# Layer-norm of the next batch in a turned layout: x also turned on the host, the row statistics sent once through DRAM, and VectorE's steps reordered

## The chip, the cores and the metric

One core of one Trainium2 chip. The metric is the device time of one execution, in microseconds (us); lower is better. Engines are named as the profile names them: PE (TensorE), DVE (VectorE), ACT (ScalarE), POOL (GpSimd), SP (SyncE, here only a DMA queue).

## What is computed

```python
def _layernorm(x, axis=-1, eps=1e-05):
    m = jnp.mean(x, axis=axis, keepdims=True)
    v = jnp.var(x, axis=axis, keepdims=True)
    return (x - m) / jnp.sqrt(v + eps)
# attention(e, q): e is the normed x, q the context of 77 rows
Sim = (e @ w1)[:, :, None] + (q @ w2)[:, None, :] + einsum('bid,bjd->bij', e * w3, q) + b_sim[0]
A = softmax(Sim, axis=2);  hq_hat = einsum('bij,bjd->bid', A, q)
Batt = softmax(max(Sim, axis=2), axis=1);  hc_bar = einsum('bi,bid->bd', Batt, e)
hcq = concat([e, hq_hat, e * hq_hat, e * hc_bar]) @ W_qv + b_qv
x = x + attention(layernorm(x), ctx)
# ffn(e): hidden = e @ W1 + b1; a sine term of hidden is added; relu; @ W2 + b2
x = x + ffn(layernorm(x))
```

x is 16 batches of 512 rows by 512 features, in float32; the FFN is 2048 wide. The first layer-norm is called LN1 here, the one before the FFN LN2.

## The kernel before, in words

A float32 product is made from three products of split operands (a high part rounded to fp32r and a low part, the rest): the PE helper `three` (L513 to L515) issues high by high, high by low and low by high. So each operand of the PE needs a high part, a copy by ACT, and a low part, a subtraction by DVE (the helper `low`, L1045).

**The pipeline over batches.** After an opening (`attention_first`) for batch 0, `body(b)` runs the FFN of batch b in 16 steps f = 0 to 15 and beside it the attention of batch n = b + 1. Each engine has a program of its own with the same loop; the order within a step is written out by hand, and semaphores tie the engines. In step f PE runs `hidden(f)` (12 matmuls of 512 columns into `hid`) and `second(f - 3)` (12 into `acc`). ACT reads `hid` twice (phase, L868; h, L871), makes the high part of the relu (L877) and the sine (L881). DVE reduces the phase (L1167, L1169), adds the sine term (`sine_term`, L1159) and makes the relu's low part (`relu_low`, L1173), which first waits for ACT's L877.

**The attention of n beside it.** Step 0 and 1: PE turns the normed rows `xin1` of batch n, 16 transposes of 128 by 128 (`tr_first`, helper line L615); ACT copies each from PSUM twice (L797 to the high part of T, L804 to `full`), DVE makes T's low part. Step 1 to 3: the context's parts, `sim_column` (L1151), and `sim` on PE ahead of `hidden(3)`. ACT adds the bias (`sim_bias`, L886) ahead of its phase of step 3, PE turns the result (`sim_rows`, L636) directly behind `hidden(3)`. Steps 4 to 7: row maxima, softmax, the row mean. Step 8: `prob_turn` on PE. At the start of step 9 ACT and DVE copy its result to `at_s` (`stack_out` L906, `second_stack_out` L1214), and PE reads it in `hq_hat(n, 0)` (L521, L522) between `hidden(9)` and `second(6)`. At step 10 PE runs `hidden(10)`, `hidden(11)` and the whole product with W_qv (`products`); DVE waits there for PE's chunks (`chunk`). Steps 11 to 15: x plus attention, statistics, LN2, eight transposes each at steps 13 and 14 (`tr_second`).

**LN1 of the batch after.** SP loads `xin1` (`xin_load`) at step 1 and X at step 6; DVE takes the statistics of n + 1 at step 3 (`stats_first`, L1058), POOL turns them into mean and 1/std (`deviation_first`, L1520 to L1532) at step 4, DVE applies them by rows at step 10 (`norm_first`, L1062).

**Queues.** POOL issues all loads of split weights (`w1_load`, `tile_load`), each behind a wait for PE; SP issues loads of x and of the context (`ctx_load`, L409), and the stores. In body 0 the weights are split for the first time: raw loads on SP, high parts by ACT (L861, L853), low parts by DVE (`w1_low`, `tile_low`), stores by POOL. There PE's `hidden(f + 2)` waits for DVE's `w1_low` of step f.

Of the kernel before, what the change touches and what calls it, by code (L numbers as in the profile page):

```python
# [37 lines left out]
P = 128  # L38
# [12 lines left out]
def xattn_ffn(nc, x, ctx_rows, w_sim, b_sim, W_qv, b_qv, W1, b1, theta, w_real, w_imag, W2, b2, out):  # L51
# [32 lines left out]
    g_dram = nc.dram_tensor("g_dram", [CN, P, C, CR], F32).ap()  # L84
    hqw_dram = nc.dram_tensor("hqw_dram", [B * J, D], F32).ap()

    with ExitStack() as ctx:
# [21 lines left out]
        X = sb("X", [P, 2, RT, D])  # L109
        xin1 = sb("xin1", [P, RT, D])  # L110
# [26 lines left out]
        e_bc = sb("e_bc", [P, R])  # L137
        hqs = sb("hqs", [P, 2, D], F32R)
# [15 lines left out]
        mv = sb("mv", [P, RT, 3]); mv_x = sb("mv_x", [P, RT, 3])  # L154
# [6 lines left out]
        rstd = sb("rstd", [P, RT]); rstd_x = sb("rstd_x", [P, RT])  # L161
# [36 lines left out]
        ctx_in = sem("ctx_in"); x1_in = sem("x1_in"); xin_in = sem("xin_in"); x_in = sem("x_in")  # L198
# [143 lines left out]
        c_product = [X[:, 1, q] for q in range(4)]  # L342

        w1q_raw, w1q = w3_sb, T[:, 1]

# [10 lines left out]
        def _(sp):  # L356
            row = lambda v, n: v.rearrange("(a d) -> a d", a=1).to_broadcast([n, D])

            def xin_load(n):

                sp.wait_ge(tr1, RT * n)
                sp.dma_start(xin1[:], x_rows[n]).then_inc(xin_in, 16)

            def x_load(n, par):

                need(sp, out_stored, 16 * (n - 1))
                sp.dma_start(X[:, par], x_rows[bass.ds(n, 1)].rearrange("b p t d -> (b p) t d")
                             ).then_inc(x_in, 16)
# [96 lines left out]
            def store(b, par):  # L465
                sp.wait_ge(b_evac, RT * (b + 1))
                sp.dma_start(out_rows[bass.ds(b, 1)].rearrange("b p t d -> (b p) t d"), X[:, par]
                             ).then_inc(out_stored, 16)

            def attention_first():  # L470
                for q in range(2):
                    sp.wait_ge(g_stored[3 + q], g_stores(3 + q, CN))
                    raw_w1_load(q)

            def body(b, par, first, last):
                n, pn = b + 1, 1 - par
                for f in range(FT):
# [14 lines left out]
                    if f == 1 and n + 1 < B:  # L492
                        xin_load(n + 1)
                    if f == 6:
                        if first:
                            for q in range(4):
                                sp.wait_ge(p_late[q], 16)
                        x_load(n, pn)

            def rest():  # L500
                for t in range(RT):
                    sp.wait_ge(b_evac, RT * (B - 1) + t + 1)
                    sp.dma_start(out_rows[B - 1, :, t], X[:, (B - 1) % 2, t]).then_inc(out_stored, 16)
# [6 lines left out]
        def _(pe):  # L510
# [107 lines left out]
            def tr_first(n, t):  # L618

                transpose_rows(n, t, xin1[:, t], xn1, tr1, (t2_lo, RT * n - 2 + t + 1) if t < 2 else (t1_lo, RT * n + t - 1))  # L620
# [77 lines left out]
            def attention_first():  # L698
                pe.wait_ge(s_ident, 1)
                turn(0)  # L700
                turn_vectors()
                turn(1)
                multiply(0)
# [25 lines left out]
                multiply(7)  # L729
                tr_second(0, 0)  # L730
# [6 lines left out]
            def body(b, par, first, last):  # L737
                n, pn = b + 1, 1 - par
                for f in range(FT):
                    if f == 3 and not last:  # L740
                        sim(n, pn)
# [31 lines left out]
                    if last:  # L773
                        continue
                    if f == NA + 3:
# [18 lines left out]
        def _(sc):  # L794
            def turned_high(n, t, par, ready, done):
                sc.wait_ge(ready, RT * n + t + 1)
                nc.scalar.copy(T[:, par, 0, :, t * P:(t + 1) * P],  # L797
                               mis[:, t % 2].rearrange("p (c r) -> p c r", c=C)).then_inc(done, 1)

# [124 lines left out]
            def attention_first():  # L924
# [41 lines left out]
                w1_high(1)  # L966
                product_copy(7)
# [67 lines left out]
        def _(ve):  # L1035
# [11 lines left out]
            def stats_first(n, t):  # L1047
# [4 lines left out]
                else:  # L1052
                    if n == 1:
                        ve.wait_ge(x1_in, 16)
                    else:
                        ve.wait_ge(xin_in, 16 * (n - 1))
                    ve.wait_ge(xn1, RT * n)
                    ve.bn_stats(st_x[:, t], xin1[:, t]).then_inc(st1, 1)  # L1058

            def norm_first(n, t):  # L1060
                ve.wait_ge(rs1, n + 1)
                ve.tensor_scalar(xin1[:, t], X[:, 0, t] if n == 0 else xin1[:, t], mv_x[:, t, 1:2],  # L1062
                                 rstd_x[:, t:t + 1], ALU.subtract, ALU.mult).then_inc(xn1, 1)
# [152 lines left out]
            def row_mean(n, chunks=range(C)):  # L1216

                for c in chunks:
                    ve.wait_ge(full_done, RT * (n + 1))
# [37 lines left out]
            def evacuate(par, t, done):  # L1257
                ve.tensor_tensor(X[:, par, t], X[:, par, t], acc[:, t], ALU.add).then_inc(done, 1)

            def attention_and_stats(n, par, tiles=range(RT)):  # L1260

                if n > 0:
                    ve.wait_ge(x_in, 16 * n)
                for t in tiles:
                    ve.wait_ge(att_done, RT * n + t + 1)
                    evacuate(par, t, x2_done)
                    ve.wait_ge(x2_done, RT * n + t + 1)
                    ve.bn_stats(st[:, t], X[:, par, t]).then_inc(st2, 1)

            def norm_second(n, par, t):  # L1270
# [3 lines left out]
                ve.tensor_scalar(xin[:, t % 2], X[:, par, t], mv[:, t, 1:2], rstd[:, t:t + 1],  # L1274
                                 ALU.subtract, ALU.mult).then_inc(xn2, 1)

            def add_b2(n, par, t):
# [3 lines left out]
                ve.tensor_tensor(X[:, par, t], X[:, par, t], b2_bc[:], ALU.add).then_inc(xb2_done, 1)  # L1281

            def add_first_part(b, par):
# [3 lines left out]
                for t in range(RT):  # L1287
                    evacuate(par, t, a_evac)

            def add_last_part(b, par, whole):  # L1290
# [6 lines left out]
                for t in range(RT):  # L1297
                    if whole:
                        ve.wait_ge(last_sum, t + 1)
                    evacuate(par, t, b_evac)  # L1300

            def attention_first():
# [11 lines left out]
                for t in range(RT):  # L1314
                    norm_first(0, t)
# [43 lines left out]
                for t in range(RT):  # L1359
                    norm_first(1, t)  # L1360
# [4 lines left out]
                for half in range(2):  # L1365
                    pair = range(2 * half, 2 * half + 2)
                    attention_and_stats(0, 0, pair)
                    variance_of(st, mv, vareps, 2 * half, 2 * half + 2, st2, ag2, va2)
                    for t in pair:
                        norm_second(0, 0, t)  # L1370
                for t in range(RT):
                    turned_low(0, t, 0, t2_hi, t2_lo)
                add_b2(0, 0, 0)
                add_b2(0, 0, 1)
                ve.wait_ge(g_stored[0], g_stores(0, CN))

            def body(b, par, first, last):
                n, pn = b + 1, 1 - par
                for f in range(FT):
                    g = FT * b + f  # L1380
                    if f == NA - 1 and not last:
                        second_stack_out(n)
# [4 lines left out]
                    if f == 1 and not last:  # L1387
                        turned_low(n, 0, pn, full_done, t1_lo)
                        turned_low(n, 1, pn, full_done, t1_lo)
                    if f == 2 and not last:  # L1390
                        turned_low(n, 2, pn, full_done, t1_lo)
                        turned_low(n, 3, pn, full_done, t1_lo)
                        g_low(n)
                        sim_column(n)
# [230 lines left out]
```

## Time and profile before

| what | value |
|---|---|
| median of 3 runs | 2024.87 us (2021.78 to 2025.04) |
| the profiled execution | 2022.12 us |
| its span, first to last instruction | 2020.3 us |
| granted TensorE clock, mean | 0.996 of full |
| busy: PE, DVE, ACT, POOL | 98%, 67%, 48%, 20% |
| DMA | 386 MB, 191 GB/s |

Two microseconds of the profiled time lie outside its span. In the views a duration is that of one instruction; instructions of PE overlap, so what one of them costs is the distance between two starts. "Idle" rows name what ended the wait.

### The profile page before, as it was taken

Reading aid. Unit: us, or ns where it says so; the run is one execution under the profiler, and the core shown is the slowest. Engines: PE = TensorE matmul, PEld = TensorE weight load, DVE = VectorE, ACT = ScalarE, POOL = GpSimd, SP = SyncE. Lnnn points to the kernel's source line nnn. Section 1 sums busy time; section 2 is a strip of 40 time slices with the busy share of each in tenths; the row PEclk is TensorE's granted clock in tenths of the full one; section 3 lists DMA queues with packets and bytes.
Section 4 is the critical chain, followed back from the end, with each engine's and each line's share of the span. In section 5 each row is a group of like instructions: output and inputs, shape, how many; then the busy total and the mean of one; then the engine's idle time right before and its main releaser. Section 6 shows DMA issues by size and latency. Waiting matters only on the chain.

```text
span 2020.3 us, 25250 instructions
## 1 busy us (share of the span) xinstructions
PE 1980.5 (98%) x9057; PEld 1626.0 (80%) x9057; DVE 1356.7 (67%) x2406; ACT 965.3 (48%) x1669; POOL 401.1 (20%) x834
## 2 busy tenths in 40 slices
PE   6989999999999999999999999999999999999999
PEld 5767788888888888888888888888888888888887
DVE  6777675767767577675767767567675767767554
ACT  7464543635445363543636445363543636445343
POOL 0122222212122121122212122121122212121110
PEclk9999999999999999999999999999999999999999
DMA  7375856757477574766757476574766756467473
GB/s 261 121 263 188 288 178 175 238 150 223 136 214 218 152 231 127 229 180 173 238 148 224 138 217 216 151 230 128 227 182 174 235 148 222 142 196 217 136 209 124
DMA packets 143679, 386.22 MB, mean 191 GB/s; under 512 B 24995, under 2 KB 34539, under 8 KB 143556
## 3 DMA queue, kind: packets, MB, share of 16 engines
q0 software_dynamic: 83584, 304.31, 49.9%
q1 hardware_dynamic: 59828, 80.27, 12.6%
q8 instruction: 73, 1.20, 0.3%
q14 instruction: 50, 0.41, 0.1%
q10 hardware_dynamic: 144, 0.04, 0.0%
HBM read 343.81 MB, written 40.76 MB: 190 GB/s over the span
## 4 chain that ended last, share of the span: by engine, by line
PE 71%; DVE 15%; ACT 7%; issue 5%; DMA 1%; SPq 0%; DVEq 0%; POOL 0%; ACTq 0%
PE acc L513 13%; PE acc L514 13%; PE acc L515 13%; PE hid L513 8%; PE hid L515 8%; PE hid L514 8%; DVE ph L1169 3%; DVE h L1159 3%; PE mis L615 3%; ACT act L877 2%; DVE kk L1167 2%; DVE st_x L1058 2%; DVE tmp_w L1221 1%; ACT L881 1%; PE mis L521 1%
## 5 line engine op out<-in xcount | busy, mean ns | idle before, releaser
L513 PE MATMUL hid<-T,w1s 128*128 128x512 f32 x1024 | 403.8, 394 | 4.9 <-DVE ws L1045 4.3
L513 PE MATMUL acc<-ws,act 128*128 128x512 f32 x1024 | 404.1, 395 | 0.0
L515 PE MATMUL hid<-T,w1s 128*128 128x512 f32 x1024 | 399.8, 390 | 0.0
L514 PE MATMUL acc<-ws,act 128*128 128x512 f32 x1024 | 399.4, 390 | 0.0
L515 PE MATMUL acc<-ws,act 128*128 128x512 f32 x1024 | 399.4, 390 | 0.0
L514 PE MATMUL hid<-T,w1s 128*128 128x512 f32 x1024 | 399.3, 390 | 0.0
L868 ACT ACTIVATE ph<-hid,hbias 128x512 f32<-128x512 f32 x256 | 176.0, 688 | 407.2 <-PE hid L515 407.2
L877 ACT ACTIVATE act<-h 128x512 fp32r<-128x512 f32 x256 | 161.9, 632 | 390.6 <-DVE h L1159 369.4
L1173 DVE SCALAR_TENSOR_TENSOR act<-h,act 128x512 fp32r<-128x512 f32 x256 | 177.3, 693 | 185.7 <-ACT act L877 185.7
L1167 DVE TENSOR_SCALAR kk<-ph 128x512 f32<-128x512 f32 x256 | 108.8, 425 | 284.0 <-ACT ph L868 284.0
L1498 POOL DMA_DIRECT2D ws<-w2x_dram x240 | 127.6, 532 | 750.1 <-PE acc L515 739.8
L513 PEld LDWEIGHTS hid<-T,w1s 128*128 128x128 f32 x1024 | 192.9, 188 | 45.2 <-DVE ws L1045 4.7
L515 PEld LDWEIGHTS hid<-T,w1s 128*128 128x128 f32 x1024 | 192.5, 188 | 40.7
L515 PEld LDWEIGHTS acc<-ws,act 128*128 128x128 f32 x1024 | 192.5, 188 | 40.4
L514 PEld LDWEIGHTS hid<-T,w1s 128*128 128x128 f32 x1024 | 192.9, 188 | 38.8
L1492 POOL DMA_DIRECT2D w1s<-w1x_dram x240 | 129.5, 539 | 475.6 <-PE hid L515 460.0
L513 PEld LDWEIGHTS acc<-ws,act 128*128 128x128 f32 x1024 | 192.8, 188 | 38.4
L514 PEld LDWEIGHTS acc<-ws,act 128*128 128x128 f32 x1024 | 192.8, 188 | 38.3
L1159 DVE SCALAR_TENSOR_TENSOR h<-ph,camp,h 128x512 f32<-128x512 f32 x256 | 190.9, 746 | 0.0
L1169 DVE TENSOR_TENSOR ph<-ph,kk 128x512 f32<-128x512 f32 x256 | 177.3, 693 | 8.8
L871 ACT ACTIVATE h<-hid,cols 128x512 f32<-128x512 f32 x256 | 174.6, 682 | 0.0
L881 ACT ACTIVATE ph<-ph 128x512 f32<-128x512 f32 x256 | 157.9, 617 | 0.2
(172 smaller groups left out, 2760.2 us busy)
## 6 DMA issues: line engine op xcount, KB each, us to landing
w1s<-w1x_dram POOLq DMA_DIRECT2D x240, 512.0 KB, 4.5
ws<-w2x_dram POOLq DMA_DIRECT2D x240, 512.0 KB, 4.0
ws<-wqx_dram POOLq DMA_DIRECT2D x56, 512.0 KB, 4.5
X<-in_x SPq DMA_DIRECT2D x15, 1024.0 KB, 8.7
out_x<-X SPq DMA_DIRECT2D x15, 1024.0 KB, 4.6
xin<-in_x SPq DMA_DIRECT2D x14, 1024.0 KB, 6.8
w_raw<-in_L_ffn_W SPq DMA_DIRECT2D x32, 256.0 KB, 4.6
w1x_dram<-w1s POOLq DMA_DIRECT2D x16, 512.0 KB, 3.6
```

Of the source, the lines that this page charges most:

```text
L513: pe.matmul(dst, w_hi, m_hi, start=start, stop=False)
L514: pe.matmul(dst, w_hi, m_lo, start=False, stop=False)
L515: mm = pe.matmul(dst, w_lo, m_hi, start=False, stop=stop)
L868: nc.scalar.activation(ph[:, f % 2], hid[:, f % 2], ACT.Identity, bias=hbias[:, f:f + 1], scale=HSCALE).then_inc(t_done, 1)
L871: nc.scalar.activation(h2[:, f % 2], hid[:, f % 2], ACT.Identity, bias=b1c[:, f:f + 1], scale=1.0).then_inc(h2_done, 1)
L877: nc.scalar.activation(act[:, f % 4, 0], h2[:, f % 2], ACT.Relu).then_inc(act_hi, 1)
L881: nc.scalar.activation(ph[:, f % 2], ph[:, f % 2], ACT.Sin, scale=TWO_PI_BELOW).then_inc(s_done, 1)
L1159: ve.scalar_tensor_tensor(out=h2[:, f % 2], in0=ph[:, f % 2], scalar=camp[:, f:f + 1], in1=h2[:, f % 2], op0=ALU.mult, op1=ALU.add).then_i ...
L1167: ve.tensor_scalar(kk[:], ph[:, f % 2], ROUND, -ROUND, ALU.add, ALU.add).then_inc(k_done, 1)
L1169: ve.tensor_tensor(ph[:, f % 2], ph[:, f % 2], kk[:], ALU.subtract).then_inc(r_done, 1)
L1173: ve.scalar_tensor_tensor(out=act[:, f % 4, 1], in0=h2[:, f % 2], scalar=0.0, in1=act[:, f % 4, 0].bitcast(F32), op0=ALU.max, op1=ALU.subtract
L1492: po.dma_start(w1s[:, s].rearrange("p a c k -> p (a c k)"), w1x_dram[f % FT].rearrange("p a c k -> p (a c k)")).then_inc(w1_in[s], 16)
```

## The change

The host also hands in x turned: `in_x_turned`, per batch 128 partitions by 4 chunks by 512 rows. For n from 1 to 15 the turned x is loaded straight into `full`, and LN1 is applied there by two passes over it, `center` and `scale`; mean and 1/std vary along the free axis there. So they are sent to all partitions: PE turns the 12 columns (mean, variance, 1/std of 4 tiles) in one transpose, ACT copies them out, SP stores them to DRAM and, after a wait for that store, loads mean and 1/std as 512-element rows to all 128 partitions (`mean_bc`, `e_bc`). X has three buffers; `xin1` is gone. Batch 0 keeps its transposes, its normed rows lie in `w0_sb`, whose load moves behind them. `multiply(0)` goes ahead of `turn(1)` in the opening.

```diff
 # SP
-            def xin_load(n):
-                sp.wait_ge(tr1, RT * n)
-                sp.dma_start(xin1[:], x_rows[n]).then_inc(xin_in, 16)
+            def turned_load(n):
+                sp.wait_ge(pr_lo, C * n)
+                sp.dma_start(full[:], x_turned[n]).then_inc(xt_in, 16)
+            def spread_stats(n):
+                sp.wait_ge(srow_done, n)
+                sp.dma_start(stat_dram[n % 2], srow).then_inc(stat_st, 16)
+                sp.wait_ge(stat_st, 16 * n)
+                sp.wait_ge(hbr_done, C * n)
+                for at, dst in ((0, mean_bc[:]), (2 * RT, e_bc[:])):
+                    sp.dma_start(dst, stat_dram[n % 2, at:at + RT].rearrange("(a t) p -> a (t p)", a=1).to_broadcast([P, R])
+                                 ).then_inc(bc_in, 16)
...
                     if f == 6:
...
+                        x_load(n + 1)
+                    if f == NA + 1:
+                        turned_load(n + 1)
+                    if f == NA + 2:
+                        spread_stats(n + 1)
 # PE
+            def turn_stats(n):
+                pe.wait_ge(rs1, n + 1)
+                pe.wait_ge(prt_done, C * n)
+                pe.transpose(mis[0:3 * RT, 1, 0:P], row_x[:, 1:4].rearrange("p k t -> p (k t)"), ident[:]).then_inc(srow_t, 1)
             def tr_second(n, t):
+                if t == 1 and n + 1 < B:
+                    pe.wait_ge(srow_done, n + 1)
...
-                    if f == 3 and not last:
-                        sim(n, pn)
                     if f != NA + 1 or last:
                         hidden(b, f, par)
                     if f == 8 and not last:
                         prob_turn(n)
-                    if f == 0 and not last:
-                        tr_first(n, 0)
-                        tr_first(n, 1)
-                    if f == 1 and not last:
-                        tr_first(n, 2)
-                        tr_first(n, 3)
                     if f == 3 and not last:
-                        sim_rows(n)
-                    if f == NA - 1 and not last:
-                        hq_hat(n, 0)
+                        sim(n, pn)
...
                         second(b - 1, FT + f - LAG, False, True)
                     if last:
                         continue
+                    if f == 3:
+                        sim_rows(n)
+                    if f == NA - 1:
+                        hq_hat(n, 0)
+                    if f == NA + 2 and n + 1 < B:
+                        turn_stats(n + 1)
 # ACT
+            def spread_high(n, c, par):
+                sc.wait_ge(xs_done, 4 * n)
+                nc.scalar.copy(T[:, par, 0, c], full[:, c]).then_inc(t1_hi, 1)
+            def stat_rows(n):
+                sc.wait_ge(srow_t, n)
+                need(sc, xs_done, 4 * (n - 1))
+                nc.scalar.copy(srow, mis[0:3 * RT, 1, 0:P]).then_inc(srow_done, 1)
...
-                    if f in (1, 2) and not last:
-                        for t in (2 * f - 2, 2 * f - 1):
-                            turned_high(n, t, pn, tr1, t1_hi)
-                            full_copy(n, t)
-                    if f == 3 and not last:
-                        sim_bias(n)
+                    if f == 1 and not last:
+                        spread_high(n, 0, pn)
+                        spread_high(n, 1, pn)
...
                     if f == 1:
+                        spread_high(n, 2, pn)
+                        spread_high(n, 3, pn)
                         g_high(n)
                     if f == 2:
                         context_high(n)
+                    if f == 3:
+                        sim_bias(n)
+                    if f == NA + 2 and n + 1 < B:
+                        stat_rows(n + 1)
 # DVE
+            def center(n, half):
+                if half == 0:
+                    ve.wait_ge(xt_in, 16 * n)
+                    ve.wait_ge(bc_in, 32 * n)
+                cs = slice(2 * half, 2 * half + 2)
+                ve.tensor_tensor(full[:, cs], full[:, cs], mean_bc[:].unsqueeze(1).to_broadcast([P, 2, R]), ALU.subtract
+                                 ).then_inc(xs_done, 1)
+            def scale(n, half):
+                ve.wait_ge(xs_done, 4 * n - 1 if half else 4 * n - 2)
...
+                ve.tensor_tensor(full[:, cs], full[:, cs], e_bc[:].unsqueeze(1).to_broadcast([P, 2, R]), ALU.mult
+                                 ).then_inc(xs_done, 1)
...
                     reduce_phase(b, f)
                     if f > 0 or not first:
                         sine_term(g - 1, (f - 1) % FT)
+                    if f == NA - 2 and not last:
+                        second_stack_out(n)
...
                     if f > 0 or not first:
                         relu_low(g - 1, (f - 1) % FT)
 # POOL
+                    if f == NA + 1 and n + 1 < B:
+                        deviation_first(n + 1)
                     weights(b, f, first, last)
...
-                    if f == 4 and n + 1 < B:
-                        deviation_first(n + 1)
```

DVE's new order within a step, where the diff is long: behind `sine_term` and ahead of `relu_low` now come, step by step, `scale` (0), `sim_column` and two `spread_low` (1), `add_b2` (3 and 4, all four tiles), `prob_low` and `row_mean` (6), `row_mean` and `context_low` (7), `second_stack_out` and `w0_chunk` (8), `pr_chunk` (10), `center` of n + 1 (15), and in body 0 all `w1_low` and `tile_low`. Step 2 begins with `g_low` and the other two `spread_low`. `stats_first` moves from step 3 to step 10, between the chunks; `norm_first` by rows is left for batch 0 alone. In body 0 the product additions of steps 0 and 1 (four in all) move to step 3.

## Rows read from the trace of the kernel before

**Rows 1.** The page, busy time: us, share, instructions of each engine
```profile
PE 1980.5 (98%) x9057; PEld 1626.0 (80%) x9057; DVE 1356.7 (67%) x2406; ACT 965.3 (48%) x1669; POOL 401.1 (20%) x834
```

**Rows 2.** Chain that ended last, 930 to 1130 us: start, us, engine, tile, line
```profile
939.22 0.87 PE mis L615 x8
...
954.62 0.87 PE mis L615 x8
...
1060.52 0.87 PE mis L615 x8
```

**Rows 3.** Timeline of PE, steps 8 and 9 of one body
```profile
1007.02 0.39 PE L513 MATMUL hid<-T,w1s 128*128 128x512 f32 x1
...
1009.52 0.39 PE L515 MATMUL hid<-T,w1s 128*128 128x512 f32 x1
1010.18 0.50 PE L521 MATMUL mis<-at_s,hqs 128*128 128x512 f32 x1 [0.28 <-DVE at_s L1214]
1010.52 0.39 PE L522 MATMUL mis<-at_s,hqs 103*128 103x512 f32 x1
```

**Rows 4.** Waits of PE, whole run: us in total, times, longest
```profile
PE mis L521 <- DVE at_s L1214: 9.7, 14, 6.1
...
PE hid L513 <- DVE ws L1045: 4.3, 1, 4.3
PE mis L513 <- DVE gs L1045: 3.6, 1, 3.6
...
PE mis L615 <- DVE T L1045: 2.5, 3, 2.1
```

**Rows 5.** Waits of PE from 226 us on, same columns
```profile
PE mis L521 <- DVE at_s L1214: 3.6, 13, 0.3
```

**Rows 6.** Timeline of DVE, step 3 of one body
```profile
976.30 0.43 DVE L1167 TENSOR_SCALAR kk<-ph 128x512 f32<-128x512 f32 x1 [1.88 <-ACT ph L868]
976.76 0.69 DVE L1169 TENSOR_TENSOR ph<-ph,kk 128x512 f32<-128x512 f32 x1
977.37 0.75 DVE L1159 SCALAR_TENSOR_TENSOR h<-ph,camp,h 128x512 f32<-128x512 f32 x1
978.82 0.69 DVE L1173 SCALAR_TENSOR_TENSOR act<-h,act 128x512 fp32r<-128x512 f32 x1 [0.70 <-ACT act L877]
979.43 2.47 DVE L1058 BATCH_NORM_STATS2 st_x<-xin 128x6 f32<-128x512 f32 x4
```

**Rows 7.** Timeline of ACT, steps 2 and 3 of the same body
```profile
971.22 0.62 ACT L881 ACTIVATE ph<-ph 128x512 f32<-128x512 f32 x1
971.74 0.61 ACT L845 CAST hqs<-ctx_raw 128x512 fp32r<-128x512 f32 x1
...
974.31 0.69 ACT L886 ACTIVATE tmp_w<-mis,vj 77x512 f32<-77x512 f32 x1
975.58 0.69 ACT L868 ACTIVATE ph<-hid,hbias 128x512 f32<-128x512 f32 x1 [0.59 <-PE hid L515]
976.17 0.68 ACT L871 ACTIVATE h<-hid,cols 128x512 f32<-128x512 f32 x1
978.16 0.63 ACT L877 ACTIVATE act<-h 128x512 fp32r<-128x512 f32 x1 [1.31 <-DVE h L1159]
```

**Rows 8.** Groups of DVE by shape: count, busy us, mean ns, idle before
```profile
L1045 DVE TENSOR_TENSOR T<-mis,T 128x512 fp32r<-128x512 f32 x128 | 84.7, 688 | 32.3 <-ACT full L804 21.4 <-ACT T L797 10.8
...
L1200 DVE TENSOR_TENSOR prob<-prob,rrec 128x308 f32<-128x308 f32 x16 | 7.7, 479 | 0.6
```

**Rows 9.** DMA issues: queue, count, KB each, median us to landing
```profile
X<-in_x SPq DMA_DIRECT2D x15, 1024.0 KB, 8.7
...
w_bc<-in_L_xattn_w_sim SPq DMA_DIRECT2D x1, 256.0 KB, 9.1
...
g_dram<-kk SPq DMA_DIRECT2D x1, 252.0 KB, 9.0
```

**Rows 10.** Timeline of ACT, step 12 of the same body
```profile
1046.95 0.69 ACT L868 ACTIVATE ph<-hid,hbias 128x512 f32<-128x512 f32 x1 [8.44 <-PE hid L515]
```

**Rows 11.** Stretches of body 0: PE, PEld, DVE, ACT, POOL busy, clock, DMA
```profile
106.00:110.00 4.00, 4.00 (x12) 2.62 (x11) 2.94 (x5) 3.27 (x7) 0.62 (x2) 0.59 1.01 326
...
222.00:226.00 4.00, 3.51 (x10) 2.84 (x11) 0.28 (x1) 0.00 (x0) 1.61 (x3) 0.59 0.75 241
```

More of the change, by code:

```diff
@@ L729, in attention_first @@
                 multiply(7)
+                turn_stats(1)
                 tr_second(0, 0)
@@ L1366, in attention_first @@
                     pair = range(2 * half, 2 * half + 2)
[L1367 removed]
+                    attention_and_stats(0, pair)
                     variance_of(st, mv, vareps, 2 * half, 2 * half + 2, st2, ag2, va2)
                     for t in pair:
[L1370 removed]
+                        norm_second(0, t)
                 for t in range(RT):
                     turned_low(0, t, 0, t2_hi, t2_lo)
[L1373 to L1374 removed]
+                for half in range(2):
+                    center(1, half)
                 ve.wait_ge(g_stored[0], g_stores(0, CN))
@@ L1386, in body @@
                         chunk_low(n, 0)
-                    if f == 1 and not last:
-                        turned_low(n, 0, pn, full_done, t1_lo)
-                        turned_low(n, 1, pn, full_done, t1_lo)
                     if f == 2 and not last:
-                        turned_low(n, 2, pn, full_done, t1_lo)
-                        turned_low(n, 3, pn, full_done, t1_lo)
                         g_low(n)
-                        sim_column(n)
+                        spread_low(n, 2, pn)
+                        spread_low(n, 3, pn)
                     if f == 4 and not last:
@@ L1407, in body @@
                         sine_term(g - 1, (f - 1) % FT)
+                    if f == NA - 2 and not last:
+                        second_stack_out(n)
+                    if first and f == 3:
+                        for k in range(GAP, CN):
+                            product_add(k)
+                    if first and f < FT - 2:
+                        w1_low(f + 2)
+                    if f == 0 and not last:
+                        scale(n, 0)
+                        scale(n, 1)
+                    if f == 1 and not last:
+                        sim_column(n)
+                        spread_low(n, 0, pn)
+                        spread_low(n, 1, pn)
@@ new lines, in body @@
+                    if f == FT - 1 and n + 1 < B:
+                        center(n + 1, 0)
+                        center(n + 1, 1)
+                    if f == 3:
+                        add_b2(b, 0)
+                        add_b2(b, 1)
+                    if f == 4:
+                        add_b2(b, 2)
+                        add_b2(b, 3)
+                    if f == 6 and not last:
+                        prob_low(n)
+                        row_mean(n, range(0, C // 2))
+                    if f == 7 and not last:
+                        row_mean(n, range(C // 2, C))
+                        context_low(n)
@@ L1408, in body @@
+                    if f == NA - 2 and not last:
+                        w0_chunk(n, 0)
+                    if f == NA and not last:
+                        pr_chunk(n, 1)
+                    if first:
+                        for p in splits(f, last)[0:1] if f == NA else splits(f, last):
+                            tile_low(p)
+                    if f > 0 or not first:
                         relu_low(g - 1, (f - 1) % FT)
                     if f == 2 and not first:
-                        add_last_part(b - 1, pn, False)
@@ L1411, in body @@
-                    if first and f < 2:
-                        product_add(GAP + 2 * f)
-                        product_add(GAP + 2 * f + 1)
-                    if first and f < FT - 2:
-                        w1_low(f + 2)
-                    if f == NA + 1 and first:
-                        for p in splits(f, last):
-                            tile_low(p)
-                    if f == 0:
-                        add_b2(b, par, 2)
-                        add_b2(b, par, 3)
+                        add_last_part(b - 1, False)
@@ L1461, in body @@
                         turned_low(n, 3, pn, t2_hi, t2_lo)
-                    if f not in (NA, NA + 1) and first:
-                        for p in splits(f, last):
-                            tile_low(p)
             def rest():
@@ L1581, in body @@
                         w1_store(f + 2)
-                    if first and f < 2:
-                        for k in range(GAP + 2 * f, GAP + 2 * f + 2):
+                    if first and f == 3:
+                        for k in range(GAP, CN):
                             late_product_out(k)
@@ L1619 @@
         args.append(nc.dram_tensor(f"in_{name}", a.shape, _mybir.dt.from_np(a.dtype), kind="ExternalInput").ap())
+    a = _np.asarray(inputs['x'])
+    a = _np.ascontiguousarray(a.reshape(a.shape[0], a.shape[1], -1, P).transpose(0, 3, 2, 1))
+    arrays["in_x_turned"] = a
+    args.append(nc.dram_tensor("in_x_turned", a.shape, _mybir.dt.from_np(a.dtype), kind="ExternalInput").ap())
     shape = inputs['x'].shape
```

138 lines of the change are left out of this document (63 added, 75 removed).

## Prediction

> **What bounds the kernel now.** I read the page first: PE is busy 98% of the span, DVE 67%, ACT 48% [rows 1]. A change has to shorten PE's own work or a wait of PE; relief of the others is worth nothing unless they end such a wait. The chain of waits gives the period: the same transposes of step 13 start at 939.22 and 1060.52, so a body takes 121.3 us [rows 2]. There are 14 full bodies of this kind (b = 1 to 14), body 0 before them and a last one without attention. Then PE's waits: 36 us in all, but from 226 us on only one kind is left, 13 times `at_s`, 0.3 us each [rows 4, 5]. The rest lies in the opening and in body 0 (6.1, 4.3, 3.6 and 2.1 us) [rows 4].
>
> **Prices on PE.** 11 steps from 1007.02 to 1009.52 make 0.227 us for a matmul of 512 columns, so `hidden` or `second` (12 of them) is 2.72 us [rows 3]. Eight transposes take 0.87 us, 0.109 each [rows 2]. That is the distance of starts. The Trainium skill (TensorE: Matmul & The Clock Gate, PE-mode transpose) gives about 275 ns for one transpose in a kernel; the sum by that price would take 4.4 us from each body and not 1.74, some 37 us more in all, and is too large if transposes overlap, as the row says.
>
> **The change part by part, for one body of the 14.**
>
> 1. The 16 transposes of `tr_first` go: 16 x 0.109 = **-1.74 us**. They are on PE's path in full, nothing waits there at that time [rows 5].
>
> 2. One transpose of 12 columns comes (`turn_stats`, step 12). The trace has none of this shape; between nothing and one full transpose with a refill of 0.2, I take **+0.11** (its moving side is the same 128 columns). Its waits are long over: statistics are taken between the chunks of step 10, where DVE is idle, and POOL's eight small instructions follow before step 12. Behind `deviation_first` on POOL now stand a W1 load and the four tile loads of step 11, some of which leave up to 9 us later; they are read from step 12 on. Its ACT copy waits some 5 us inside step 12, where ACT's next work is `hidden(13)`, later still.
>
> 3. The wait for `at_s` goes. PE is free at 1009.52 + 0.227 = 1009.75, L521 starts at 1010.18, and the next start is 0.34 behind it where 0.23 is normal: 0.43 + 0.11 = **-0.54 us** [rows 3]. Now `second(6)` (2.72 us) stands ahead of `hq_hat(n, 0)`, and `second_stack_out` is a step earlier, so some 4 us of slack are there.
>
> 4. DVE: relu_low stands idle for 0.70 us in nearly every step, waiting for ACT's L877 [rows 6]. The new order fills that gap with other work. In the full bodies this moves no PE work by itself; it is slack.
>
> 5. `center` and `scale`, two instructions each of 128x1024. One DVE instruction of 512 takes 0.69 us with starts 0.60 apart, one of 308 takes 0.48 [rows 8]; the slope is 1.02 ns per element, so 1024 elements cost 1.14 from start to start, with 0.6 (if twice the rate) and 2.3 (if half) as ends. I take 1.14: two of them 2.3 us in step 15 and 2.3 in step 0. Against them 4 `norm_first` are gone. DVE has the room on average.
>
> 6. The path of the statistics through DRAM. ACT's phase of step 12 starts at 1046.95 [rows 10]. PE is done with three `second` 8.2 us later, at 1055; store at 1055.6; `center` comes in step 15, behind `hidden(13)`, `second(10)`, 8 transposes, `hidden(14)`, `second(11)`, 8 transposes, `hidden(15)` and DVE's reduce and sine term, at about 1073. So 17 us stand ready for a store, a wait and two loads of 256 KB. The nearest rows, in the crowded opening, are 9.0 and 9.1 us [rows 9]: 19 us at worst, 5 or 6 if the queues are free. I take no cost: behind `center` on DVE stands `relu_low(14)`, which PE needs only in the next step 1, 5 us after its usual time. x turned (1 MB, 8.7 us [rows 9]) is asked for at the end of step 10 and has 30 us. `ctx_load` is now queued behind this on SP, some 14 us later than before, and still 20 us ahead of its use.
>
> 7. **The new wait.** Here I expect a part of the gain to be given back. Let A be ACT's start of the phase, step 0 at A = 0. By PE alone steps follow at 5.44 (two times 2.72). DVE: kk 0.72 after the phase, sine term at 1.79, two `scale` from 2.45 to 4.8. ACT's `spread_high` waits for both, so two copies (0.52 each) end at 5.85 and the phase of step 1 starts 0.4 late. From there: DVE's sine term at 7.66, relu high part 0.78 later at 8.44 [rows 6, 7], sine, two more `spread_high`, `g_high` from 10.54; DVE's `g_low` at 11.05, two `spread_low`, and only at 12.66 kk of step 2, one us late. Then, with distances of rows 6 and 7: relu high part at 14.51, sine, four context copies (2.57 us) to 18.14, the phase of step 3 (PE has had it ready since 16.3, since `sim` no longer stands ahead of `hidden(3)`), kk 18.86, sine term 19.93, relu high part 20.71, sine, and now `sim_bias` last, 21.77 to 22.46. PE has by then run `second(15)`, `hidden(3)`, `sim` (12 matmuls, 2.78) and `second(0)` and is at `sim_rows` at 21.78. It waits 0.72, and refilling costs the 0.11 of point 3: **+0.83 us**. Ends: none, if DVE or ACT gain 0.7 anywhere on this line, and 2 us if each instruction between is 5% dearer. I take the middle because every term is from a row.
>
> Sum for a body: -1.74 + 0.11 - 0.54 + 0.83 = -1.34 us; 14 times, **-18.8 us**.
>
> **Opening and body 0.** In the opening PE's `multiply(0)` fills a DMA wait, but ACT's parts of `turn(1)` come some 2 us later; the w0 load leaves later and w3's earlier. Ends -2 and +3, taken as 0. Body 0 is bound by DVE up to step 9. It loses 16 transposes and the 6.1 us at `at_s` [rows 4], since the relu gap of 0.7 us in some seven steps is filled and `at_s` is wanted later; but the same line as in point 7 makes PE wait at `sim_rows` some 5 us, and body 0 has shown that waits of 3.6 and 4.3 us are followed by four microseconds at a granted clock of 0.59, mostly at the lower of the two levels (1.2 GHz) [rows 4, 11]. The skill's same page warns of this in its table of goals, to avoid long idle gaps between bursts of matmuls; rows 11 agree. Following DVE's list step by step I get `products` of body 0 some 4.5 us earlier. The last wait (4.3 us, a tile's low part in step 15) stays: two `center` take the place of `relu_low` and two `add_b2` ahead of it, and SP's raw loads wait 3 us behind `spread_stats`. Together **-4 us**, ends -12 and +5.
>
> Total: 2022.12 (the profiled execution) - 18.8 - 4 = 1999.3. The median shown lies 2.7 us above that execution; runs spread over 3.3 us. I say **2000 us**.
>
> **Rivals.**
> - *The wait at `sim_rows` doesn't appear.* For it: 0.7 us is small beside a line of 22 us. Against: every duration is from a row. Then each body gives 2.17, 14 make 30.4, and with -4 the time is **1988**.
> - *Slower: `scale` is dear.* Place: step 0, in front of `spread_high`. Each us there is a us at `sim_rows`. The gain of a body is gone when that wait costs 2.17, so when two `scale` take 1.34 us more, 1.8 us apiece. At half rate (2.3 each) the cost is 3.15, a body loses 1.0 and the time is 2022 + 14 - 4 = **2032**. Against: an operand spread by a step of 0 is there already in prob by rrec and costs no more than its like [rows 8].
> - *The statistics are late.* If store and loads take over 17 + 5 us, PE waits at `second(14)`. At 24 us a body loses 2, in all 1999 + 28 = **2027**; it would need both transfers above the worst rows.
> - *Body 0 gives it back.* Idle and half clock outweigh: +5 and not -4, **2009**.
> - *A transpose costs its duration*, 0.27 and not 0.109: 37 us more, **1963**. The starts in the chain deny it [rows 2].
>
> **Chances.** The forecast 0.50; no wait at `sim_rows` 0.22; body 0 gives it back (or the wait is nearer 1.5) 0.17; scale dear or another new wait of DVE 0.05; statistics late 0.05; transposes dearer 0.01. The measurement tells about 0.2%, 4 us, from no change. Range: 1984 (no wait, body 0 at -8) to 2013 (wait of 1.5, body 0 at 0). Faster by over 0.2% 0.91, within 0.03, slower 0.06.
>
> **What would show it.** Right: `tr_first` and `tr_second` together with 272 transposes, not 512, and 15 of `turn_stats`; in a full body the period near 120.0; no wait for `at_s`; instead PE's `sim_rows` waiting for ACT's `sim_bias`, 14 times near 0.7 us; `center` with no wait for DMA; DVE's `relu_low` idle far below 186 us. Wrong: a period of 119.1 (no wait) or above 121.3 (then look in step 0 for `scale`, in step 15 for `center`, whichever PE's waits name); a granted clock under 1.0 beyond body 0; body 0 with waits above its 16 us of now [rows 4].

## The result, and the profile after

The changed kernel takes **2014.04 us** (median of 6 runs, 2011.35 to 2016.04) against 2023.74 (6 runs, 2021.78 to 2025.12): ratio 0.9952, 95% interval 0.9940 to 0.9964. It is faster by 9.7 us. The forecast was 2000, some 24 us less than before; the sign is right, the size less than half, and the time lies 1 us outside the range. Taken apart, the full bodies did what was forecast, and body 0 did not.

The page, busy time (the answer to [rows 1]), and the group of DVE's `relu_low`:

```profile
PE 1958.3 (97%) x8832; PEld 1602.5 (80%) x8832; DVE 1393.0 (69%) x2406; ACT 938.3 (47%) x1624; POOL 386.5 (19%) x834
...
L1229 DVE SCALAR_TENSOR_TENSOR act<-h,act 128x512 fp32r<-128x512 f32 x256 | 176.1, 688 | 83.9 <-ACT act L911 82.5
```

PE has 225 instructions fewer (240 `tr_first` out, 15 `turn_stats` in). The idle time in front of `relu_low` fell from 185.7 to 83.9 us. That is slack won by DVE, and by itself no time.

The chain, the same transposes of step 13 in two bodies in a row (the answer to [rows 2]):

```profile
939.31 0.88 PE mis L635 x8
...
1059.36 0.87 PE mis L635 x8
```

A body takes 120.05 us, 1.25 less than 121.30; 1.34 was forecast. PE's waits from 226 us on (the answer to [rows 5]) say what limits it now:

```profile
PE mis L664 <- ACT tmp_w L920: 10.4, 14, 0.7
PE hid L533 <- DVE ws L1083: 3.2, 1, 3.2
```

The 13 waits for `at_s` are gone. In their place `sim_rows` (L664) waits for ACT's `sim_bias` (L920), 14 times and 10.4 / 14 = 0.74 us each, where 0.72 was forecast. Now PE's waits of the whole run (the answer to [rows 4]):

```profile
PE mis L664 <- ACT tmp_w L920: 15.3, 15, 4.9
PE hid L533 <- DVE w1s L1083: 8.0, 3, 5.5
PE mis L635 <- DVE xin L1331: 5.2, 1, 5.2
```

In body 0 there are three waits of about 5 us. The 4.9 at `sim_rows` was expected. The other two are new: `hidden` waiting for `w1s`, and `tr_second` waiting for `xin`. The starts of PE show what they make. First the kernel before, then the changed one: the first instruction of body 0's `hidden(0)`, the first of body 1's, and the last matmul of all.

```profile
88.06 0.40 PE L513 MATMUL hid<-T,w1s 128*128 128x512 f32 x1
...
222.49 0.77 PE L513 MATMUL hid<-T,w1s 128*128 128x512 f32 x1 [4.28 <-DVE ws L1045]
...
2016.64 0.39 PE L515 MATMUL acc<-ws,act 128*128 128x512 f32 x1
```

```profile
89.68 0.39 PE L533 MATMUL hid<-T,w1s 128*128 128x512 f32 x1
...
231.25 0.47 PE L533 MATMUL hid<-T,w1s 128*128 128x512 f32 x1 [3.16 <-DVE ws L1083]
...
2007.33 0.39 PE L535 MATMUL acc<-ws,act 128*128 128x512 f32 x1
```

These lines make the whole ledger. Opening: 89.68 - 88.06 = +1.6. Body 0: 141.57 against 134.43, **+7.1**. Bodies 1 to 15: 1776.08 against 1794.15, **-18.1**. From the last matmul to the end of the span: 5.27 against 3.66, +1.6. The sum is -7.7, the difference of the spans (2012.6 against 2020.3). PE's marked waits between the first two of these starts add up to 22.0 us, against 17.0 before, and the mean granted clock there is 0.94, against 0.96.

**Why body 0 is longer.** PE's long wait of 5.46 us is at 100.75. Followed back it leads through DVE and ACT to a raw load on SP. SP's queue, with the ACT and PE instructions behind it:

```profile
71.12 0.34 SPq L372 DMA_DIRECT2D full<-in_x_turned  x1
82.41 0.32 SPq L377 DMA_DIRECT2D stat_dram<-mean_bc  x1
83.72 0.33 SPq L381 DMA_DIRECT2D mean_bc<-stat_dram  x1
84.09 0.44 SPq L381 DMA_DIRECT2D e_bc<-stat_dram  x1
84.57 0.43 SPq L431 DMA_DIRECT2D w_raw<-in_L_ffn_W  x1
85.25 2.04 SPq L423 DMA_DIRECT2D tmp_w<-g_dram  x2
...
90.72 1.13 SPq L439 DMA_DIRECT2D w_raw<-in_L_ffn_W  x2
```

```profile
99.36 0.62 ACT L895 CAST w1s<-w_raw 128x512 fp32r<-128x512 f32 x1 [5.48 <-DMA w_raw<-in_L_ffn_W]
```

```profile
100.75 0.80 PE L533 MATMUL hid<-T,w1s 128*128 128x512 f32 x1 [5.46 <-DVE w1s L1083]
```

In the kernel before, `raw_w1_load(2)` was issued at 81.41, its high part began at 92.19, and nobody waited for the load:

```profile
77.75 1.28 SPq L409 DMA_DIRECT2D tmp_w<-g_dram  x2
...
81.41 0.94 SPq L425 DMA_DIRECT2D w_raw<-in_L_ffn_W  x2
```

```profile
92.19 0.62 ACT L861 CAST w1s<-w_raw 128x512 fp32r<-128x512 f32 x1
```

Now it is issued 9.3 us later. The eight issues of `ctx_load` stood ahead of it in the kernel before too, from 77.75 to 81.41. Now they begin 7.5 us later, at 85.25, and take 5.5 us and not 3.7, until 90.72; these two parts are the 9.3. What holds them back is `spread_stats(1)` in front of them. After `turned_load` at 71.12 SP issues nothing until the statistics are there at 82.41. Then come their store, 1 us of waiting for it, the two broadcast loads, and `raw_tile_load(0)` at 84.57, which left at 64.17 in the kernel before. The load itself then takes 8.6 us (90.72 to 99.36), where the median of the 32 raw loads is 4.6. The same happens once more at step 12: `spread_stats(2)`, with 2.4 us of waiting for its store, stands ahead of `raw_w1_load(15)`, which leaves at 207.81. ACT waits 7.13 us for it, and everything behind it on ACT is late:

```profile
214.30 0.62 ACT L895 CAST w1s<-w_raw 128x512 fp32r<-128x512 f32 x1 [7.13 <-DMA w_raw<-in_L_ffn_W]
```

```profile
220.11 1.97 PE L635 MATMUL mis<-ident,xin 128*128 128x128 f32 x8 [5.15 <-DVE xin L1331]
```

Behind such waits PE runs at the lower of its two levels for a while (the answer to [rows 11]; columns: stretch, length, busy time of PE, PEld, DVE, ACT, POOL, granted clock, DMA share, GB/s):

```profile
106.00:110.00 4.00, 2.65 (x6) 2.15 (x7) 3.96 (x10) 3.27 (x7) 0.53 (x1) 0.63 0.32 131
...
122.00:126.00 4.00, 3.13 (x10) 2.64 (x11) 4.00 (x8) 0.82 (x2) 2.15 (x5) 0.50 0.27 109
```

### The profile page after: what moved, and what is told of

Its sections match the earlier page's. It is cut to its first block, busy times and chain, and to the rows that moved or that the text cites. A ratio compares the mean times of both kernels' runs of the same rounds, so it can differ in the third digit from the quotient of the medians.

```text
span 2012.6 us, 24724 instructions
## 1 busy us (share of the span) xinstructions
PE 1958.3 (97%) x8832; PEld 1602.5 (80%) x8832; DVE 1393.0 (69%) x2406; ACT 938.3 (47%) x1624; POOL 386.5 (19%) x834
## 4 chain that ended last, share of the span: by engine, by line
PE 74%; DVE 12%; ACT 6%; issue 4%; DMA 3%; SPq 1%; ACTq 0%; DVEq 0%
PE acc L535 14%; PE acc L533 14%; PE acc L534 14%; PE hid L533 9%; PE hid L535 9%; PE hid L534 9%; DVE h L1215 2%; DVE T L1083 2%; DVE ph L1225 2%; DVE full L1109 2%; DMA w_raw<-in_L_ffn_W 2%; ACT ph L902 2%; DVE kk L1223 1%; PE mis L635 1%; ACT ph L915 1%
## 5 line engine op out<-in xcount | busy, mean ns | idle before, releaser
L1229 DVE SCALAR_TENSOR_TENSOR act<-h,act 128x512 fp32r<-128x512 f32 x256 | 176.1, 688 | 83.9 <-ACT act L911 82.5
```

The source lines that it names most:

```text
L1229: ve.scalar_tensor_tensor(out=act[:, f % 4, 1], in0=h2[:, f % 2], scalar=0.0, in1=act[:, f % 4, 0].bitcast(F32), op0=ALU.max, op1=ALU.subtract
```

## The experiments

Each kernel was timed against the kernel before on its own chip: a median of 2023.41 us for the first four, 2024.12 for the last four. The ratios and intervals are worked out from all runs, so they are not quite the quotients of the medians. "Hidden(0) to hidden(0)" means the stretch of body 0 as in the ledger, 134.4 us before and 141.6 after.

### 1. ScalarE's bias earlier (ratio 0.9875)

```diff
                     phase_and_hidden(b, f)
+                    if f == 3 and not last:
+                        sim_bias(n)
...
-                    if f == 3:
-                        sim_bias(n)
```

> The changed kernel with sim_bias moved on ACT from the end of step 3 to right behind phase_and_hidden(3). Theory (in the full bodies PE waits at sim_rows only because sim_bias is last in ACT's step 3, some 0.83 us per body with the refill): sim is done about 1 us before ACT has issued both readings of hid, so sim_rows finds its input; the wait of 0.74 us on L664 vanishes in all 14 bodies, the period falls from 120.05 to 119.2, and with a shorter wait in body 0 (4.9 now) the time is 11 to 16 us below the changed kernel. Rival (ACT as a whole is late there, the place of sim_bias is not what counts): the wait moves to hidden(4) or to spread_max, and the period stays at 120.

Measured: **1999.81 us** (1998.47 to 2000.75), interval 0.986 to 0.989. The chain and ACT's bias in one full body:

```profile
933.27 0.87 PE mis L635 x8
...
1052.39 0.87 PE mis L635 x8
```

```profile
968.10 0.68 ACT L920 ACTIVATE tmp_w<-mis,vj 77x512 f32<-77x512 f32 x1
```

The period is 119.12. From 226 us on PE waits once, for a `ws` tile at the start of body 1, and never at `sim_rows`. So the wait of 0.74 us cost 0.93 with its refill (120.05 - 119.12), in each full body. The 14.2 us between this kernel and the changed one are inside the 11 to 16 that were expected; of the 13.7 by which the spans differ, 11.9 lie behind the start of body 1 and 2.3 in body 0. The order of ACT's step 3, not the work in it, made the wait.

### 2. The raw loads of body 0 ahead of the statistics (ratio 0.9924)

```diff
                 turned_load(1)
+                raw_tile_load(0)
+                raw_w1_load(2)
+                raw_w1_load(3)
                 spread_stats(1)
...
                     if f == NA + 2:
+                        if first:
+                            raw_w1_load(FT - 1)
                         spread_stats(n + 1)
```

> The changed kernel; on SP alone, raw_tile_load(0), raw_w1_load(2) and raw_w1_load(3) are issued ahead of spread_stats(1), and raw_w1_load(15) ahead of spread_stats(2), all in the opening and body 0. Theory (body 0 is 7 us longer than before because raw weight loads stand on SP's queue behind the round trip of the statistics and the context loads pushed behind it): PE's wait of 5.5 us at hidden(2) goes, the one of 5.2 us in step 14 shrinks by 3 to 4 us, time 7 to 12 us below the changed kernel; the period of 120.05 does not change. Rival (body 0 is longer because DVE has more to do there, scale and center): the waits move behind scale and center, and the time stays within 2 us.

Measured: **2010.08 us** (2006.69 to 2011.51), interval 0.9907 to 0.9940, 4 us under the changed kernel, where 7 to 12 had been expected. The wait of 5.46 us is gone; the next `hidden` waits 3.59 where it had waited 2.26. The wait in step 14 is 4.27 in place of 5.15: the hoisted load still stands behind the raw tile loads of step 12. Body 0 is 137.7 us, 3.8 less. The raw loads are confirmed as a cause, with about half of the 7.1 us; their size was put too high.

### 3. turn(1) ahead of multiply(0) in the opening (ratio 0.9935)

```diff
-                multiply(0)
                 turn(1)
+                multiply(0)
```

> The changed kernel with turn(1) ahead of multiply(0) on PE again, as before. Theory (the opening is 1.6 us longer because ACT's parts of turn(1), and all behind them, start later): hidden(0) starts near 88 and not 89.7, 1 to 2 us less in all. Rival (the opening is longer through the later w0 load or the product buffers): hidden(0) stays at 89.7 or comes later, since PE then stands idle at turn(1) again.

Measured: **2012.64 us** (2010.36 to 2013.65), interval 0.9918 to 0.9952. `hidden(0)` starts at 87.27 and not 89.68, but the times overlap with the changed kernel's, and experiment 4, whose opening is that of before, began it at 89.75, 1.7 later than the kernel before. Experiment 5, which has this order too, began it at 90.61. The opening varies by as much as this edit could bring: inconclusive.

### 4. The kernel before with the move at step 8 and 9 alone (ratio 0.9948)

Here the edit is made on the kernel before: `hq_hat(n, 0)` goes behind `second(6)`, `second_stack_out` into step 8.

```diff
-                    if f == NA - 1 and not last:
-                        hq_hat(n, 0)
...
+                    if f == NA - 1:
+                        hq_hat(n, 0)
 # DVE
                         sine_term(g - 1, (f - 1) % FT)
+                        if f == NA - 2 and not last:
+                            second_stack_out(n)
```

> The kernel before, with one part of the change alone: hq_hat(n, 0) behind second(6) on PE and second_stack_out in step 8 behind the sine term on DVE. Theory: the 13 waits of 0.3 us at at_s go (0.54 us per body with the refill), the period falls from 121.3 to 120.76, 7.6 us over 14 bodies; in body 0 the wait of 6.1 us goes for the most part and some of it comes back as waits for w1s or act, so 10 to 15 us below the kernel before. Rival (DVE is behind there anyway, the wait only moves to second(7) or to products): period unchanged.

Measured: **2014.80 us** (2013.98 to 2014.97), interval 0.9934 to 0.9963. The chain:

```profile
935.82 0.87 PE mis L615 x8
...
1056.60 0.87 PE mis L615 x8
```

The period is 120.78, 0.52 under 121.30; 0.54 was forecast for this part. These two moved lines on PE and DVE give as much as the whole change, which pays in body 0 for what its transposes save. Body 0 is 131.0 us here, 3.5 shorter than before. The medians differ by 8.6 us, where 10 to 15 had been expected; the interval reaches from 7.5 to 13.4. Beside experiment 1, which has no wait at `sim_rows` either, it isolates the transposes: 120.78 - 119.12 = 1.66 us a body, where 1.74 - 0.11 = 1.63 was forecast.

### 5. All four moves together (ratio 0.9836)

Experiments 1, 2 and 3, with `raw_w1_load(15)` now ahead of the raw tile loads of step 12, and `scale(1)` taken from step 0 of body 0 into the opening:

```diff
+                        if f == NA + 2:
+                            raw_w1_load(FT - 1)
                         for p in splits(f, last):
...
+                for half in range(2):
+                    scale(1, half)
...
-                    if f == 0 and not last:
+                    if f == 0 and not last and not first:
```

> The changed kernel with four moves together: sim_bias right behind phase_and_hidden(3); raw_tile_load(0), raw_w1_load(2) and (3) issued on SP ahead of spread_stats(1), and raw_w1_load(15) ahead of the raw tile loads of step 12; turn(1) ahead of multiply(0); and scale(1) of both halves in the opening, behind center(1), instead of in step 0 of body 0. Theory (what was missing is the wait at sim_rows in 14 bodies, and SP's late raw loads with VectorE's long step 0 in body 0): the period is 119.1 as in the run with the bias alone, 120.05-119.12 = 0.93 x 14 = 13.0 less than the changed kernel; body 0 is 4 to 10 shorter, both waits of about 5 us at the first hidden tiles and in step 14 gone; 1987 to 1997 in all. Rival (the opening and body 0 are bound by the spread of the clock and by what the runs leave to chance): no better than the run with the bias alone, 1999 to 2001.

Measured: **1991.89 us** (5 runs, 1988.35 to 1993.11), interval 0.9822 to 0.9849, 22 us under the changed kernel. This is inside the 1987 to 1997 that were expected. The period is 119.12; body 0 runs from 90.61 to 219.51, 128.9 us, 12.7 less than in the changed kernel. Its two new waits were expected to go: they fell to 2.2 us (at `hidden(3)`) and 1.5 (in step 14).

### 6. One more VectorE instruction in step 0 (ratio 1.0143)

```diff
+                        ve.wait_ge(xs_done, 4 * n - 2)
+                        link(ve.tensor_tensor(full[:, 0:2], full[:, 0:2], full[:, 0:2], ALU.max))
```

> The changed kernel with one more VectorE instruction of 128x1024 (full max full, into itself; the values stay) ahead of the scaling in step 0 of each body. It prices VectorE's step 0 against the wait at sim_rows. Theory of the prediction (each us in step 0 is a us at sim_rows, since the bias stands behind the context copies, and those behind VectorE's kk): the wait at sim_rows of 0.74 becomes 1.8 to 2.0, the period 120.05 becomes 121.1 to 121.3, and the time 2014 + 14 x 1.14 = 2030, 2026 to 2034. Rival (VectorE catches up before kk of group 1, or ScalarE's copies are not what ends last): the wait stays under 1, the period within 0.2 of 120.05, and the time 2012 to 2018.

Measured: **2053.50 us** (2051.13 to 2054.36), interval 1.0129 to 1.0157. Neither expectation held: it costs 39 us, not 16. PE's waits from 226 us on:

```profile
PE mis L664 <- ACT tmp_w L920: 28.0, 14, 2.0
```

The wait grew to 2.0 us, by 1.26 for an instruction of 1.22 us: that is the price the theory gave. But the period is 122.93, 2.88 more:

```profile
957.55 0.88 PE mis L635 x8
...
1080.48 0.88 PE mis L635 x8
```

The rest stands in the granted clock (the columns are those of the stretches above). First this kernel, one full body, then the changed kernel at the same place:

```profile
994.00:996.80 2.80, 0.80 (x5) 0.34 (x3) 2.79 (x5) 1.72 (x3) 0.53 (x1) 1.00 0.87 320
996.80:998.00 1.20, 1.20 (x7) 1.01 (x8) 0.64 (x2) 0.00 (x0) 0.00 (x0) 0.66 0.95 280
998.00:1000.00 2.00, 2.00 (x6) 1.61 (x5) 0.31 (x1) 0.00 (x0) 0.00 (x0) 0.50 0.69 207
```

```profile
974.00:978.00 4.00, 3.25 (x18) 2.42 (x17) 3.43 (x7) 1.95 (x4) 0.53 (x1) 1.00 0.74 278
978.00:982.00 4.00, 4.00 (x19) 3.28 (x18) 1.41 (x4) 1.27 (x2) 0.53 (x1) 1.00 0.97 322
```

Behind the wait of 2.0 us PE falls to 1.2 GHz until about 1000.5, its matmuls 0.43 us apart and not 0.23; behind 0.74 us the clock stays at 2.4 GHz. From `sim_rows` to `spread_max` the same work takes 7.45 us and not 5.83. So 1.26 of wait and 1.62 of clock make the 2.88.

One full body confirms this split. In body 1 the wait is as long, but the clock does not fall:

```profile
260.81 0.49 PE L664 MATMUL mis<-ident,tmp_w 77*128 77x77 f32 x4 [1.97 <-ACT tmp_w L920]
```

```profile
258.00:262.00 4.00, 2.03 (x12) 1.43 (x11) 3.44 (x7) 1.72 (x3) 0.53 (x1) 1.00 0.92 301
262.00:266.00 4.00, 4.00 (x20) 3.27 (x19) 1.42 (x4) 1.27 (x2) 0.53 (x1) 1.00 0.81 261
```

The next body's `sim_rows` starts at 382.15, 121.34 us later. That is 1.29 more than 120.05, the longer wait alone. In the other 13 bodies the clock falls. A wait of 2.0 us thus costs 3.8 where the clock falls (122.93 - 119.12, the period without a wait).

### 7. hq_hat(n, 0) back in its old place (ratio 0.9960)

```diff
+                    if f == NA - 1 and not last:
+                        hq_hat(n, 0)
...
-                    if f == NA - 1:
-                        hq_hat(n, 0)
```

> The changed kernel with hq_hat(n, 0) put back to where it stood before, ahead of second(6); VectorE's new order stays. It tells whether moving hq_hat did it or the earlier second_stack_out. Theory A (the stack's copies are now issued in time, so the wait on at_s does not come back): period 120.05 within 0.1, no wait on at_s over 0.1 from 226 on, time 2014 within 2. Theory B (the place of hq_hat is what removed the wait): the wait of 0.43 comes back in every body, period 120.5, time 2020 within 2.

Measured: **2016.38 us** (2013.49 to 2018.25), interval 0.9947 to 0.9974. DVE's copy of the stack, for which PE had waited, then ACT's, and their first reader, in one full body:

```profile
1005.98 0.68 DVE L1270 CAST at_s<-mis 103x512 fp32r<-103x512 f32 x1
```

```profile
1007.15 0.57 ACT L940 CAST at_s<-mis 128x512 fp32r<-128x512 f32 x1
```

```profile
1009.67 0.39 PE L541 MATMUL mis<-at_s,hqs 128*128 128x512 f32 x1
```

Theory A holds: no wait is marked, DVE's copy is done at 1006.66 and ACT's at 1007.72, two microseconds early, and the period is 120.05. The time is 2.3 us above the changed kernel's, where at most 2 had been expected, and the intervals overlap. In the full bodies DVE's earlier copy, in step 8, removed the wait; the later place of the reader was not needed. In body 0 this kernel waits 3.0 us for `at_s` and the changed one 0.3, but body 0 as a whole is only 0.4 us longer (141.9).

### 8. The moves of body 0 alone (ratio 0.9910)

Experiment 5 without the early bias and with `multiply(0)` where the change put it.

> The changed kernel with the moves of body 0 alone: raw_tile_load(0), raw_w1_load(2) and (3) ahead of spread_stats(1), raw_w1_load(15) ahead of step 12's raw tile loads, scale(1) in the opening. No change to sim_bias. Theory (SP's queue and VectorE's step 0 are what body 0 lost): the stretch from the first hidden(0) to that of the next body falls from 141.6 to between 130 and 137, the period stays 120.05, the time is 2003 to 2009. Rival (the raw loads are paid elsewhere, only the earlier run's 4 us come): 2009 to 2012.

Measured: **2005.80 us** (2004.24 to 2007.73), interval 0.9896 to 0.9923, 8 us under the changed kernel. The time and body 0 are both where they were expected (2003 to 2009, and 130 to 137): `hidden(0)` stands at 88.88, that of body 1 at 221.45, 132.6 us, 9.0 less. The second wait, in step 14, is 2.31:

```profile
210.30 1.11 PE L638 MATMUL mis<-ident,xin 128*128 128x128 f32 x8 [2.31 <-DVE xin L1334]
221.45 0.47 PE L536 MATMUL hid<-T,w1s 128*128 128x512 f32 x1 [4.55 <-DVE ws L1086]
```

The period is 120.06 (930.98 to 1051.04), as it should be. Two of these edits are SP's and one is DVE's; experiment 2 has the first part of SP's alone (3.8 us), the other 5 us are not split between the higher place of `raw_w1_load(15)` and the earlier `scale`.

## Why the prediction was half right

- **Points 1 and 2, transposes out, one in: right.** Forecast -1.63, measured -1.66 by experiments 1 and 4. The Trainium skill's 275 ns for a transpose (TensorE: Matmul & The Clock Gate, PE-mode transpose) would have made 4.4; in the after trace too the median duration is 272 ns, while eight of them still take 0.87 us.
- **Point 3, at_s: right in size (-0.52), half right in cause.** DVE's earlier copy did it, without the later place of `hq_hat` (experiment 7).
- **Point 5, center and scale: right.** They last 1.22 us, starts 1.13 to 1.25 apart, where 1.14 was taken; the two passes neither ran at twice nor at half rate.
- **Point 6, the way through DRAM: right for the full bodies.** The broadcast loads landed in 4.1 and 6.7 us, x turned in 8.6, and `center` waited once for a DMA, 0.9 us.
- **Point 7, the wait at sim_rows: right.** 0.74 us and 0.93 in all, against 0.72 and 0.83 (the two times of the prediction, 22.46 and 21.78, differ by 0.68, a slip of no weight). Removed, the kernel gains 14 us. The same wait in body 0 was forecast as some 5 us and came as 4.9; with the bias early it fell to 0.4, and body 0 became 2.3 us shorter.
- The sum for a body was -1.34, measured -1.25; from body 1's start to the last matmul -18.1 against -18.8.
- **Opening: inside its ends.** +1.6 against 0 (-2 to +3). Experiment 4 shows the same shift without the change, so this +1.6 can't be laid to it.
- **Body 0: this is the step that failed.** -4 was forecast, +7.1 came, just beyond the end of +5: 11.1 of the 15.1 us by which the forecast span (2020.3 - 22.8 = 1997.5) was off. The text named the place, "SP's raw loads wait 3 us behind `spread_stats`", but only as a reason why the last wait stays, with no cost of its own. What the runs show instead: the issue was 9.3 us later, since `spread_stats(1)` held back `ctx_load` and with it all that follows on SP; the reader (ACT's high part of step 2) had no such slack, so PE waited 5.46 us. At step 12 the hold was near the 3 us of the text (204.15 to 206.93), but it made a new wait of 5.15 us in step 14. PE's waits in body 0 are 22.0 us, above the 16 that the prediction had named as a sign of being wrong. Moving raw loads alone gave back 3.8 us (experiment 2), all moves of body 0 together 9.0 (experiment 8). With the loads moved and `scale` early, body 0 takes 132.6 against 130.4 forecast. In point 6 the later `ctx_load` was followed to its own reader, and not to what is queued behind it on SP.
- **The tail: not a term of the change.** 1.6 us more lie between the last matmul and the end of the span. In the traces of the kernel before and of experiments 2, 4, 6, 7 and 8 this stretch is 3.6 to 3.7 us, in those of the changed kernel and of experiments 1, 3 and 5 it is 5.3 to 5.9. Only these four have, behind the last stores, one more packet of 0.02 MB on the DMA queue that the profile calls `instruction`. That the span ends later because of it is likely, but no run isolates it.
- **The range.** Its upper end, 2013, took body 0 at 0, although the prediction had given +5 as the end of that term. With +5 the range would have held the time.
- The rival "body 0 gives it back" (+5, 2009, 0.17) named the right part and the nearest time. "No wait at `sim_rows`" is what experiment 1 made: at 1999.8 and not 1988, as body 0 is still the changed one.
- The rival "`scale` is dear" was priced one us for one us. Experiment 6 shows that 1.2 us more in step 0 would have cost 2.9 a body and ended slower: the rival's price was too low by the clock's part, and the 2032 worked out with it left that part out.

## What to carry to other kernels

When a step is moved or put on a DMA queue, list everything behind it with its reader's slack, once for each place where it is issued, the rare iterations included; an issue with a wait in it belongs behind the loads that an engine is about to need. An engine that ends a tight line (here ACT's bias) goes ahead of work with slack in the same step. A wait on PE costs little more than its length while the clock stays (0.93 us for 0.74), and close to twice its length where the clock falls (3.8 for 2.0).

## What the runs showed of the hardware beyond that

- In 13 of 14 full bodies of experiment 6 a wait of 2.0 us, inside a stretch where PE was otherwise busy without a gap, was followed by some 3.5 us at 1.2 GHz, worth 1.6 us; the 14 waits of 0.74 us in the changed kernel never were. In experiment 5 the wait of 1.92 us at `sim_rows` in body 0 was followed by four microseconds at a granted clock of 0.62 as well. The Trainium skill's page "TensorE: Matmul & The Clock Gate" (table of goals under "Why this matters for your kernels") warns of long idle gaps between bursts of matmuls; the gap that was enough here is shorter than the waits of 3.6 and 4.3 us from which the prediction had it.
- The length of a wait alone does not decide. Body 1 of experiment 6 waited 1.97 us and kept the full clock. The changed kernel waited 3.16 us at 231.25 and kept it too, while 2.92 us at the same place in experiment 1 were followed by matmuls 0.43 us apart. What decides between them stays open.

```profile
231.00:235.00 4.00, 3.75 (x17) 3.14 (x18) 0.66 (x3) 0.74 (x2) 1.61 (x3) 1.00 0.65 214
```

- The same eight issues of `ctx_load` took 3.7 us of SP's queue in the kernel before (77.75 to 81.41) and 5.5 us in the changed one (85.25 to 90.72), and nothing behind them left meanwhile.
